# Cross-attention and FFN layer on one core: preparation in 64-row matmul pairs, second batch's parts later

## The reference, cut to what matters

```python
def reference(x, ctx, Wq, Wk, Wv, Wo, bo, gamma, beta, fc1_q, fc1_s, b1, fc2_q, fc2_s, b2):
    # x (2, 1024, 256), ctx (2, 77, 192), 8 heads of 64, all float32
    h = layernorm(x)
    q, k, v = heads(h @ Wq), heads(ctx @ Wk), heads(ctx @ Wv)   # Wq (256, 512), Wk and Wv (192, 512)
    x = x + merge(softmax(q @ k.T / 8) @ v) @ Wo + bo            # Wo (512, 256)
    w1 = (fc1_q - 128) * fc1_s          # (256, 1024), a scale for each 128 rows and column
    w2 = (fc2_q - 128) * fc2_s          # (1024, 256)
    h = layernorm(x) * gamma + beta
    return x + 0.5 * (silu(h @ w1 + b1) @ w2 + b2)
```

## Time and profile before

| | |
|---|---|
| median of 3 runs | 190.82 us (190.44 to 191.01) |
| the profiled execution | 190.24 us |
| its span, first to last instruction | 188.5 us |
| busy: PE, DVE, ACT, POOL | 182.1, 123.5, 122.6, 115.6 us |
| instructions of PE (matmuls) | 1502 |

### The profile page before, as it was taken

The page is one execution under the profiler, slowest core; times in us unless marked ns, Lnnn a source line. Parts: engine busy times, 40 slices in busy tenths (PEclk is TensorE's granted clock), DMA queues, the critical chain, the costliest instruction groups (busy, mean ns, idle before and its releaser), DMA issues.

```text
span 188.5 us, 3884 instructions
## 1 busy us (share of the span) xinstructions
PE 182.1 (97%) x1502; PEld 178.2 (95%) x1502; DVE 123.5 (66%) x261; ACT 122.6 (65%) x230; POOL 115.6 (61%) x159
## 2 busy tenths in 40 slices
PE   7999899799899999999999999999999999999994
PEld 7999699699899999999999999999999999998994
DVE  0287988999879374946496459746693768165341
ACT  3287970699728980898288935895389718952580
POOL 5032998479984976298709971697359753767020
PEclk9999999999999999999999999999999999999999
DMA  6996990000000100010001000100000000100101
GB/s 166 331 403 171 354 349 14 2 0 3 2 0 0 59 0 0 3 56 0 3 0 56 3 0 0 47 16 0 3 27 29 0 3 0 56 3 0 56 3 56
DMA packets 9480, 10.72 MB, mean 57 GB/s; under 512 B 2268, under 2 KB 8183, under 8 KB 9335
## 3 DMA queue, kind: packets, MB, share of 16 engines
q1 hardware_dynamic: 8837, 9.70, 15.4%
q10 hardware_dynamic: 626, 0.79, 1.4%
HBM read 8.38 MB, written 2.10 MB: 56 GB/s over the span
## 4 chain that ended last, share of the span: by engine, by line
PE 70%; DVE 10%; POOL 8%; DMA 7%; SPq 2%; issue 1%; ACT 0%
PE H L831 21%; PE T L843 21%; PE S L798 11%; PE T L819 11%; DMA s_sb<-in_L_ffn_fc_scales 7%; PE S L805 3%; PE S L751 3%; POOL w_lo L320 3%; POOL q_sb L315 3%; DVE w_lo L627 2%; DVE hT_lo L609 2%; POOL probs L278 1%; DVE q_sb L621 1%; POOL rstd L289 1%; DVE probs L567 1%
## 5 line engine op out<-in xcount | busy, mean ns | idle before, releaser
L310 POOL TENSOR_TENSOR y_lo<-y,y_hi 128x512 fp32r<-128x512 f32 x28 | 37.6, 1364 | 2.9 <-ACT y_hi L430 2.8
L278 POOL TENSOR_TENSOR probs<-probs,rsum 128x616 f32<-128x616 f32 x16 | 19.1, 1217 | 32.1 <-DVE rsum L579 32.0
L831 PE MATMUL H<-hT_hi,w_hi 128*128 128x256 f32 x128 | 37.3, 291 | 1.3 <-issue 0.8
L843 PE MATMUL T<-w_hi,y_hi 128*128 128x256 f32 x128 | 36.6, 286 | 0.6 <-DVE w_lo L627 0.6
L831 PE MATMUL H<-hT_lo,w_hi 128*128 128x256 f32 x128 | 35.5, 277 | 0.0
L843 PE MATMUL T<-w_lo,y_hi 128*128 128x256 f32 x128 | 35.5, 277 | 0.0
L831 PE MATMUL H<-hT_hi,w_lo 128*128 128x256 f32 x128 | 35.4, 277 | 0.0
L843 PE MATMUL T<-w_hi,y_lo 128*128 128x256 f32 x128 | 35.4, 277 | 0.0
L426 ACT ACTIVATE y<-H,vec 128x256 f32<-128x256 f32 x64 | 26.5, 467 | 8.1 <-PE H L831 8.1
L399 ACT ACTIVATE probs<-probs,rstd 128x616 f32<-128x616 f32 x16 | 12.9, 807 | 27.2 <-DVE probs L567 27.2
L831 PEld LDWEIGHTS H<-hT_hi,w_hi 128*128 128x128 f32 x128 | 24.1, 188 | 2.1 <-issue 1.2
(11 more groups left out here) (127 smaller groups left out, 462.0 us busy)
## 6 DMA issues: line engine op xcount, KB each, us to landing
q_sb<-in_L_ffn_fc_q SPq DMA_DIRECT2D x2, 1024.0 KB, 8.1
out_x<-x_sb SPq DMA_DIRECT2D x16, 128.0 KB, 1.8
x_sb<-in_x SPq DMA_DIRECT2D x7, 256.0 KB, 8.3
s_sb<-in_L_ffn_fc_scales SPq DMA_DIRECT2D x2, 512.0 KB, 11.8
s_sb<-in_L_ffn_fc_scales SPq DMA_DIRECT2D x1, 1024.0 KB, 7.9
wq_sb<-in_L_xattn_Wq SPq DMA_DIRECT2D x1, 512.0 KB, 5.5
wo_sb<-in_L_xattn_Wo SPq DMA_DIRECT2D x1, 512.0 KB, 8.2
wk_sb<-in_L_xattn_Wk ACTq DMA_DIRECT2D x1, 384.0 KB, 4.2
```

The costliest lines, as they stand in the source:

```text
L278: nc.gpsimd.tensor_tensor(p, p, rsum[:, j, :].unsqueeze(2).to_broadcast([P, HEADS, J]), ALU.mult).then_inc(norm_done, 1)
L310: nc.gpsimd.tensor_tensor(y_lo[:, two, :], y[:, two, :], f32(y_hi[:, two, :]), ALU.subtract).then_inc(y_lo_done, 1)
L831: ins = mm(r[:, q * W:(q + 1) * W], wt[:, c, m * P:(m + 1) * P], ht[:, c, :], start=i == 0, stop=i == len(steps) - 1)
L843: ins = mm(o, yt[:, m, j * P:(j + 1) * P], wt[:, m, :], start=m == 0 and i == 0, stop=m == M - 1 and i == 2)
```

## The change

It redoes the preparation and reorders four lists. (1) K and V: the context is transposed in three parts of 64 columns that lie on both halves of the partitions (its first 64 columns are loaded a second time), and `project` runs two 64-row matmuls side by side, one for each half of the columns of Wk or Wv. (2) The keys of M, VW and the probabilities lie by parity of heads, so `make_vw` becomes five pairs of 64-row matmuls and one 128-row matmul for the chunk in the middle (`make_middle_vw`). (3) PE's list: Wq's transposes come ahead of K, V behind `make_m(0, c)`, the scores of pair 0 ahead of VW, and of batch 1 `make_vw` goes behind HT0, the middle chunk behind AO1.1 and `make_m(1, 1)` into the loop at a = 2. (4) All transfers of weights go through SP's queue. (5) w1 is made by halves of the columns, `fc1` runs the first 128 rows for both of its column blocks and then the second 128, and `fc1(a, 0)` starts on the first half of `split_h(a)`; `fc2(0, 0)` starts on the first half of w2. (6) POOL's list is reordered, with the residual's part of `rsqrt2(0)` behind `normalize(1, 1)`, and the last `add_b2` but one waits for HT7.

```diff
-    order = [("ctxT0", "T0"), ("ctxT1", "H1"), ("K0", "T1"), ("K1", "H0"), ("WQ0", "H1"), ("WQ1", "T0"), ("XT0", "S1"), ("V0", "T1"), ("V1", "H0"),
...
+    order = [("ctxT0", "S0"), ("ctxT1", "S1"), ("WQ0", "H1"), ("WQ1", "T0"), ("K0", "T1"), ("K1", "H0"), ("XT0", "S1"),
...
+        order += [("M1.23", "S0")] * (a == 2)
...
-                sp.dma_start(ctx_sb[:, :, :], ctx_v).then_inc(ctx_in_sem, 16)
+                sp.dma_start(ctx_sb[:, :, 0:DC], ctx_v).then_inc(ctx_in_sem, 16)
+                sp.dma_start(ctx_sb[:, :, DC:DC + CC], ctx_v[:, :, 0:CC]).then_inc(ctx_in_sem, 16)
                 sp.dma_start(wq_sb[:, :, :], wq.rearrange("(n p) f -> p n f", p=P)).then_inc(wq_in, 16)
-                sp.dma_start(wv_sb[:, :, :], wv.rearrange("(n p) f -> p n f", p=CC)).then_inc(wv_in, 16)
+                for g in range(2):
+                    sp.dma_start(wk_sb[g * DH:(g + 1) * DH, :, :], wk.rearrange("(n p) f -> p n f", p=CC)[:, :, g * 2 * P:(g + 1) * 2 * P]).then_inc(wk_in, 16)
+                sp.dma_start(x_sb[:, pair(0), :], x_v[:, pair(0), :]).then_inc(x_in[0], 16)
+                for g in range(2):
+                    sp.dma_start(wv_sb[g * DH:(g + 1) * DH, :, :], ...).then_inc(wv_in, 16)
...
-                for n in range(2 * C - 1):
-                    dequantize_w1(n)
+                pool.wait_ge(s1_in[0], 16)
+                dequantize_w1(0)
                 normalize(0, 0)
                 normalize(0, 1)
-                dequantize_w1(2 * C - 1)
-                for n in range(2 * C):
-                    lower_w1(n)
+                pool.wait_ge(s1_in[1], 16)
+                dequantize_w1(1)
+                dequantize_w1(2)
+                dequantize_w1(3)
+                lower_w1(0)
                 rsqrt1(1)
-                rsqrt2(0)
+                rsqrt2_hn(0)
+                lower_w1(1)
+                lower_w1(2)
+                lower_w1(3)
+                normalize(1, 0)
+                normalize(1, 1)
+                rsqrt2_residual(0)
                 pool.wait_ge(b2_done, 1)
                 for a in range(1, NA):
...
                     for p in range(HP):
+                        if p == (2 if a == 1 else 0) and a < LAST:
+                            rsqrt1(a + 1)
                         lower_y(a - 1, p)
-                    rsqrt2(a)
+                    rsqrt2_hn(a)
+                    rsqrt2_residual(a)
+                    if a == LAST:
+                        wait_freed(pool, f"HT{LAST}")
                     add_b2(a - 1)
...
-                    ins.then_inc(freed[place[f"HT{a}"][0]], 1)
+                        ins.then_inc(h_half_split if c == 0 else freed[place[f"HT{a}"][0]], 1)
...
                 invert_sums(1, 0)
                 invert_sums(1, 1)
-                vw_lo_part(1, 1)
-                vw_lo_part(1, 2)
-                stats1(2)
                 dve.wait_ge(q2_in, 16)
                 dve.wait_ge(s2_in, 16)
                 dequantize_w2(0)
+                vw_lo_part(1, 0)
+                vw_lo_part(1, 1)
                 dequantize_w2(1)
                 prob_lo(1, 0)
                 prob_lo(1, 1)
+                stats1(2)
                 lower_w2(0)
                 lower_w2(1)
                 add_attention(1, 0)
                 add_attention(1, 1)
+                vw_lo_part(1, 2)
...
+                    for q in range(2):
+                        for i in range(3):
+                            for g in range(2):
+                                rows = slice(g * DH, (g + 1) * DH)
+                                ins[g] = mm(rs[g][:, q * BJ:(q + 1) * BJ], weight[rows, (i + g) % 3, q * P:(q + 1) * P], ctxT[rows, i, :], start=i == 0, stop=i == 2)
...
+                    for both in zip(*steps, strict=True):
+                        for m, k, e in both:
...
+                            rows = slice(e * DH, (e + 1) * DH)
...
+                            ins = mm(rs[e][:, q * D:(q + 1) * D], v_window(k, e, b, m)[rows, :], wo_sb[rows, k, :], start=k == ks[0], stop=k == ks[-1])
...
                     if p == 0:
-                        wait_freed(pe, f"HT{f}")
+                        pe.wait_ge(h_half_split, f + 1)
...
+                        if p == 0 and c == 1:
+                            wait_freed(pe, f"HT{f}")
...
-                warm(8)
+                warm(6)
                 pe.wait_ge(ident_ready, 1)
-                pe.wait_ge(ctx_in_sem, 16)
+                pe.wait_ge(ctx_in_sem, 32)
...
                 transpose_wq(0)
                 transpose_wq(1)
+                pe.wait_ge(wk_in, 32)
+                wait_freed(pe, "ctxT0")
+                wait_freed(pe, "ctxT1")
+                project("K", wk_sb)
                 x_transposes(0)
...
                 for c in range(C):
                     make_m(0, c)
+                pe.wait_ge(wv_in, 32)
+                project("V", wv_sb)
+                scores(0, 0)
+                scores(0, 1)
                 pe.wait_ge(wo_in, 16)
...
+                make_vw(0)
+                make_middle_vw(0)
                 x_transposes(1)
                 make_m(1, 0)
                 pe.wait_ge(probs_ready, 1)
                 prob_transposes(0, 0)
-                make_m(1, 1)
                 prob_transposes(0, 1)
-                make_vw(1, 0)
                 attention_out(0, 0)
                 attention_out(0, 1)
                 scores(1, 0)
                 scores(1, 1)
                 h_transposes(0)
-                make_vw(1, 1)
-                make_vw(1, 2)
-                pe.wait_ge(w1_split, 2 * C)
+                make_vw(1)
+                pe.wait_ge(w1_split, C)
                 fc1(0, 0)
                 fc1(0, 1)
+                pe.wait_ge(w1_split, 2 * C)
+                fc1(0, 2)
                 prob_transposes(1, 0)
                 prob_transposes(1, 1)
-                fc1(0, 2)
                 fc1(0, 3)
                 attention_out(1, 0)
                 attention_out(1, 1)
+                make_middle_vw(1)
                 x_transposes(2)
-                pe.wait_ge(w2_split, 2)
                 fc2(0, 0)
...
                     attention_out(a, 1)
+                    if a == 2:
+                        make_m(1, 1)
```

More of the change, by code:

```diff
@@ L1 @@
+import itertools
 import math
@@ L44, in build_program, with key_at, heads_in @@
     BJ = B * J
-    CC = DC // 2
+    CC = DC // 3
     W = UT * P
     HP = M // 2
-    VSTEP = 2 * B * P + PAIR - P
+    VSTEP = 2 * P - 52
+    VLEFT = 103
     assert B == 2 and K == 4 and C == 2 and M == 8 and JC == 5 and NA == 8
-    assert HEADS * DH == INNER and D == 2 * P and CC <= P and 2 * BJ <= BANK and HALF <= BANK and 0 < BIAS_ROW < P
-    chunk0 = [k * PAIR // P for k in range(K)]
-    assert all(chunk0[k] == k and (k + 1) * PAIR <= (chunk0[k] + 2) * P for k in range(K))
+    assert HEADS * DH == INNER and D == 2 * P and CC == DH and 2 * BJ <= BANK and HALF <= BANK and 0 < BIAS_ROW < P
+    def key_at(k, e):
+        return e * HALF + (k + e) % K * J
+    def heads_in(m):
+        return [(k, e) for k, e in itertools.product(range(K), range(2)) if key_at(k, e) < (m + 1) * P and key_at(k, e) + J > m * P]
+    assert [{e for k, e in heads_in(m)} for m in range(JC)] == [{0}, {0}, {0, 1}, {1}, {1}] and {k for k, e in heads_in(2)} == {K - 1}
     assert s1.shape[0] == C and s2.shape[0] == M
@@ L98, in build_program @@
         q2_sb = sb("q2_sb", [P, M, D], I32)
-        s1_sb = sb("s1_sb", [P, C, F])
+        with nc.sbuf_tensor("s1_sb", [P, C, F], F32) as s1_sb:
+            pass
+        y = sb("y", [P, M, W])
         s2_sb = sb("s2_sb", [P, M, D])
@@ L387, in place_v @@
                     two = slice(2 * n, 2 * n + 2)
+                    nc.scalar.activation(v_cols[0:DH, two, :, 0:J], r[0:DH, :, :, :], ACT.Copy)
                     nc.scalar.activation(v_cols[DH:P, two, :, J:PAIR], r[DH:P, :, :, :], ACT.Copy).then_inc(freed[place[name][0]], 1)
@@ L485, in _ @@
                 prob_hi(1, 1)
-                for n in range(2):
-                    half = slice(n * M // 2, (n + 1) * M // 2)
-                    act.wait_ge(w2_done, n + 1)
-                    nc.scalar.activation(w2_hi[:, half, :], w2_sb[:, half, :], ACT.Copy).then_inc(w2_hi_done, 1)
+                split_w2(0)
                 hidden(0, 2)
+                split_w2(1)
                 hidden(0, 3)
                 nc.scalar.activation(table_probe[:, :], neg_half[:, 0:1], ACT.Exp)
+                vw_hi_part(1, 2)
                 x_hi(2)
@@ L517, in _, with stats1 @@
             def _(dve):
-                def stats1(a):
+                def stats1(a, js=range(UT)):
                     dve.wait_ge(x_in[a], 16)
-                    for t in range(a * UT, (a + 1) * UT):
+                    for t in (a * UT + j for j in js):
                         nc.vector.bn_stats(bn1[:, t, :], x_sb[:, t, :]).then_inc(bn1_done, 1)
@@ L790, in scores @@
                         wait_freed(pe, f"XT{a}")
-                        if a % AB == 0:
```

(16 more changed lines are left out.)

254 lines of the change are left out of this document (130 added, 124 removed), and 6 rows, old and new, of the table order.

## The result

The changed kernel takes 195.06 us (median of 4 executions, 194.13 to 198.17) beside 190.91 for the kernel before on the same chip. The execution of 198.17 ran at a lower granted clock and is left out of the ratio, 1.0183, interval 1.0093 to 1.0274; the median of the other three is 194.79. The kernel is slower, as forecast, but 3.4 us above the 191.7 and outside the range. The profiled execution took 195.33 for a span of 193.5, against 190.24 and 188.5.

What follows compares the result with a forecast made beforehand. Bound: a preparation ending at 51.82, its stalls ended by DVE and POOL, then six passes of 19.9 of PE's work. +0.64 + 0.97 - 0.67 = +0.94 took 190.24 to 191.2, median 191.7; range 189.1 to 193.3.

Steps and rivals of the forecast that it cites:

- Stage 1: Preparation up to make_m(0, 0): its start moves from 11.49 to 10.0, with Wq at 6.6 and Wk at 7.6.
- D: At hn: POOL's next lower_w1 gets there first, hn 1.25 late, 192.2 us; chance counted within the forecast's 0.42.
- +0.97 and -0.67: make_m(1, 1) moved into pass 2 adds 0.97 in full; PE's stall in the last pass, 0.67, goes.
- Rival C: PE's clock rises late, behind Wq and half of K, costing 0.9 and 0.7 more: 193.3 us; chance 0.13.
- Stage 2: To normalize(0, 1): scores start at 13.7, POOL's two normalisations end at 23.25, before about 23.9; gain 0.65.
- Stages 3 and 4: h's transposes: 33.67 becomes 31.6; fc1(0, 0): 37.28 becomes 35.9, with h's low part waiting for a whole lower_w1.
- Stage 5: To scores(2, 0): 51.82 becomes 52.5, as POOL and DVE alternate for 14.2 up to the last y_lo.
- Stage 6: Passes and end: make_m(1, 1) adds 0.97, a last-pass stall of 0.67 goes, fc1 by halves changes no count.
- A: TensorE decides after all: POOL and DVE alternate more mildly, scores(2, 0) earlier; 188.3 us, half of it 189.7; chance 0.25.
- B: Inputs arrive early: everything up to Stage 5 shifts by up to 1.0; 190.8 us, no change; chance 0.20.

Runs made afterwards that it cites:

- e2: The changed kernel with four extra warm matmuls behind the context's transposes and eight behind Wq's, filling PE's pauses; 193.03 us, ratio 1.0105.
- e4: The kernel before with one line added: in the last pass POOL's add_b2 waits until h's last split is done; 189.92 us, ratio 0.9953.
- e10: e6 with POOL's five residual steps of pair 0 moved back ahead of lower_w1(1); 193.47 us, ratio 1.0157.
- e12: e6 with dequantize_w1(1) and (2) moved back ahead of normalize(0, 0); 192.07 us, ratio 1.0086.
- e6: The changed kernel with Wk and x of pair 0 on ACT's queue, four extra warm matmuls, and make_m(1, 1) ahead of the loop; 191.54 us, ratio 1.0039.
- e13: e12 with the copy of the context moved from SP's queue to the head of ACT's; 191.28 us, ratio 1.0030.
- e9: e6 with POOL's lower_w1(1) waiting until both halves of hn are written; 192.13 us, ratio 1.0068.
- e5: The changed kernel with Wk and x of pair 0 on ACT's queue, four extra warm matmuls, and pair 0's residual steps behind lower_y(0, 3); 193.66 us.
- e11: e4 with fc1 by halves of its contraction, starting on the first half of h; 189.43 us, ratio 0.9932.
- e14: e13 with lower_w1(1) moved ahead of rsqrt1(1), and POOL waiting for hn before lower_w1(2); 189.79 us, ratio 0.9911.

## Why the prediction was right or wrong

**Stage 1 was wrong, and it makes the miss.** `make_m(0, 0)` at 14.25 instead of 10.0 is 4.1 us at S0 (17.81 for 13.7), as much as the span of the profiled execution is too long (193.5 for 189.4). Between S0 and S2 0.4 more came than the sum's 38.8, less than D's 0.5, and behind S2 0.6 less than the +0.97 and -0.67. (Against the 191.7 the miss is 3.4, because the 0.6 from the profiled execution to the median did not come: the profiled execution was itself above the median.) Two terms failed.

The first is the landing of Wk: K started at 10.14, not 7.6, which is 2.5. "Wk 384 KB later at about 0.39 MB a us is 7.6" uses a rate that the windows do not show: 184 GB/s from 5 to 7 us and 230 from 7 to 9 (before: 356 and 300, with two queues and longer pieces). Not all of this is the change's, since e2, with the same transfers, has Wk at 8.5.

The second is the clock, put at 2.4 GHz from 5 us on: from K's start to `make_m(0, 0)` 4.1 went by, not 2.4, which is 1.7. Rival C, with a chance of 0.13, was what happened. Its price "0.9 and 0.7 more" has the right size by luck: Wq's slow transposes (the 0.9) cost nothing, because PE waited for Wk behind them anyway, and all of K ran slow, not half, for 1.6. The clock should have stood as a term, because the change makes the pauses itself: fewer warm matmuls, and two waits for transfers where the kernel before had PE at work throughout. e2 shows that filling them takes 1.5 us or more out of the total; but e4 had the clock late with no pause at all, so the pauses are not its only cause.

The Trainium skill, page "TensorE: Matmul & The Clock Gate", section "Part 1: The HAM clock gate", ties the faster clock to sustained work of PE. The traces agree in part: with the pauses filled (e2) the fast clock is there for Wq's transposes, and behind the thin stretches of e10 and e12 the granted clock falls to 0.52 and 0.50; but in e6 it was not there for Wq's transposes although PE had no pause ahead of them from 4.90 on, and e13 kept it behind the same wait as e12.

**Stage 2 held.** From the first scores to the end of `normalize(0, 1)` 9.55 was forecast and 9.78 came.

**Stages 3 and 4: sum right, place wrong.** hn's transposes came 19.47 behind S0, not 17.9; `fc1(0, 0)` then 3.02 behind them, not 4.3. The meeting of a long `lower_w1` with DVE was forecast for the split of h and happened at hn (D). The sum, 22.49 for 22.2, is right within 0.3. e9 shows that the meeting cannot simply be avoided.

The Trainium skill, page "SBUF — State Buffer", section "Who interferes with whom", says that DVE's casts contend too, which no row of before showed. e10 does: the cast of hT takes 0.88 and 1.37 where it takes 0.28 else.

**Stage 5 held in sum.** 14.2 us from the sums to the last y_lo, measured 14.2; S2 16.65 behind `fc1(0, 0)`, forecast 16.56; `fc2(0, 0)` behind `add_attention(1, 0)`, then a gap for y_lo. But the terms don't add up one by one: the residual steps, put at 2.05, give back only 0.7 when they are taken out (e5), and in e10 POOL's list is only 0.5 shorter without them, because it then waits for DVE.

**Stage 6: the two effects held, the sum did not.** Forecast were +0.97 and -0.67, together +0.30; from S2 to the end of the span it went from 136.85 to 136.55, which is -0.30. `make_m(1, 1)` cost 1.4 (e6), not 0.97, and the end without a gap gave 0.8 (e4). "That `fc1` runs by halves changes no count" was wrong: it gave 0.13 in each pass, 0.8 in all behind S2 (e11 beside e4).

**Rivals.** A and B did not occur. What A looked for, hn's transposes early, needs POOL's work out of the way: in e14 they are at 17.95 behind S0.
